# A graph kernel's second edge pass: which signal frees a ring row for the next gather

## The reference

```python
hh = (x @ W).reshape(n, H, D)                      # 8 heads of 32
s_src = jnp.einsum('nhd,hd->nh', hh, a_src)
s_dst = jnp.einsum('nhd,hd->nh', hh, a_dst)
scores = leaky_relu(s_src[src] + s_dst[dst], 0.2)
m = segment_max(scores, dst)
e = jnp.exp(scores - m[dst])
denom = segment_sum(e, dst)
msgs = hh[src] * (e / denom[dst])[:, :, None]
out = segment_sum(msgs, dst)
```

## Time and profile before

| what | value |
| --- | --- |
| median of 3 runs | 5405.28 us (5404.92 to 5430.75) |
| the profiled execution | 5400.45 us, its span 5398.4 us |
| this pass, first gather to last add | about 2797 to 4181 us of the span, 1384 us |
| busy share over the whole span | PE 73%, PEld 53%, DVE 57%, ACT 34%, POOL 46% |
| mean granted clock of TensorE | 0.844 of full speed |

### The profile page before, as it was taken

One profiled execution on the slowest core, in us unless ns is written; L12 is line 12 of the kernel. 1 busy time (PEld: TensorE's weight loads), 2 busy tenths in 40 slices (PEclk: granted clock), 3 DMA queues, 4 the chain that ended last, 5 costly groups with the idle time before them and its releaser, 6 DMA issues. The chain is left out here.

```text
span 5398.4 us, 69620 instructions
## 1 busy us (share of the span) xinstructions
PE 3959.7 (73%) x16281; PEld 2855.2 (53%) x16282; DVE 3059.0 (57%) x7623; ACT 1862.2 (34%) x5073; POOL 2462.0 (46%) x2442
## 2 busy tenths in 40 slices
PE   6867777777776659967854667666667338999999
PEld 4545555555554448856732444444444226777776
DVE  3278878778877766662063666666667773111111
ACT  1333433333333313211223444444444322333332
POOL 2256656556656450001166666666663422333332
PEclk8989988889989879987986776777777559999999
DMA  2555545455555332311173333333331451111111
GB/s 79 187 145 156 155 143 150 141 148 152 148 147 146 90 123 78 95 57 38 47 255 89 95 94 95 94 96 94 94 95 52 128 193 21 32 31 31 31 31 27
DMA packets 316127, 553.65 MB, mean 103 GB/s; under 512 B 63430, under 2 KB 213782, under 8 KB 315856
## 3 DMA queue, kind: packets, MB, share of 16 engines
q0 software_dynamic: 137120, 388.63, 26.5%
q1 hardware_dynamic: 178736, 161.98, 9.6%
HBM read 459.75 MB, written 90.62 MB: 102 GB/s over the span
## 5 line engine op out<-in xcount | busy, mean ns | idle before, releaser
L427 POOL DMA_INDIRECT attend_ring<-kv_rows,all_step_src x880 | 859.0, 976 | 630.0 <-PE attend_ps_agg L468 366.3
L942 POOL DMA_INDIRECT edge_ring<-head_rows,all_step_src x880 | 878.1, 998 | 455.6 <-issue 212.6
L978 PE MATMUL edge_ps_agg<-edge_msg,edge_sel 128*128 128x264 f32 x1760 | 727.3, 535 | 221.6 <-issue 65.4
L468 PE MATMUL attend_ps_agg<-attend_msg,attend_sel 128*128 128x264 f32 x1760 | 604.1, 445 | 188.1 <-DVE graph_qa L785 128.6
L978 PEld LDWEIGHTS edge_ps_agg<-edge_msg,edge_sel 128*128 128x128 f32 x1760 | 410.1, 259 | 373.6 <-issue 209.8
L2813 DVE TENSOR_TENSOR moe_gl<-moe_ps_h,moe_act 128x341 f32<-128x341 f32 x210 | 107.8, 514 | 776.8 <-PE moe_ps_h L2731 776.8
L452 PE MATMUL attend_ps_q<-graph_qa,attend_sel_t 128*128 x1760 | 525.8, 428 | 25.2 <-issue 25.2
L1283 DVE TENSOR_TENSOR graph_acc<-graph_acc,edge_ps_agg 128x264 f32 x880 | 369.6, 420 | 296.5 <-PE edge_ps_agg L978 195.4
L785 DVE SCALAR_TENSOR_TENSOR graph_qa<-graph_qa,all_step_same,attend_ps_agg 128x264 f32 x880 | 421.5, 479 | 176.0 <-remote 126.7
L468 PEld LDWEIGHTS attend_ps_agg<-attend_msg,attend_sel 128*128 128x128 f32 x1760 | 329.8, 209 | 352.5 <-issue 150.6
L2731 PE MATMUL moe_ps_h<-experts_w,moe_xt 128*128 x1680 | 501.8, 451 | 0.6 <-ACT moe_xt L2762 0.6
(11 more groups left out here) (424 smaller groups left out, 6470.4 us busy)
## 6 DMA issues: line engine op xcount, KB each, us to landing
attend_ring<-kv_rows,all_step_src POOLq DMA_INDIRECT x880
edge_ring<-head_rows,all_step_src POOLq DMA_INDIRECT x880
kv_rows<-qkv_kv SPq DMA_DIRECT2D x25, 512.0 KB, 2.9
experts_w<-in_w_t SPq DMA_DIRECT2D x16, 682.0 KB
attend_mask<-run_starts SPq DMA_DIRECT2D x440, 8.1 KB
edge_mask<-run_starts SPq DMA_DIRECT2D x440, 8.1 KB
head_rows<-hds_hh SPq DMA_DIRECT2D x25, 264.0 KB
qkv_x<-in_x SPq DMA_DIRECT2D x25, 256.0 KB, 3.2
```

The costliest lines, as they stand in the source:

```text
L427: nc.gpsimd.indirect_dma_start(ring[:, step % RING1, :], None, g.kv_rows, bass.IndirectOffsetOnAxis(g.step_src[:, step:step + 1], 0)).then ...
L468: nc.tensor.matmul(ps_agg[i % SUM_BANKS][:, 0:AGG], sel[:, q % 2, u % QU, :], msg[:, q % 2, u % QU, :], start=True, stop=True).then_inc(s_ ...
L942: nc.gpsimd.indirect_dma_start(ring[:, n % slots, u, :], None, g.head_rows, bass.IndirectOffsetOnAxis(g.step_src[:, step:step + 1], 0)).th ...
L978: nc.tensor.matmul(ps_agg[i % BANKS][:, 0:AGG], sel[:, q % 2, u % QU, :], msg[:, q % 2, u % QU, :], start=True, stop=True).then_inc(s_agg, 1)
```

## The change

In front of a gather whose row was used before, POOL waits for the count of messages of DVE instead of the count of sums of PE, with the same number, that of the step whose row it takes.

```diff
                 for u in range(CH):
                     step = n * CH + u
                     if n >= slots:
-                        pool.wait_ge(s_agg, step - slots * CH + 1)
+                        pool.wait_ge(s_msg, step - slots * CH + 1)
                     nc.gpsimd.indirect_dma_start(ring[:, n % slots, u, :], None, g.head_rows,
```

## The result

The changed kernel takes 5600.64 us, median of 4 runs (5578.69 to 5612.46), against 5410.62 for the kernel before (4 runs, 5404.92 to 5430.75): a ratio of 1.033, 95% interval 1.0307 to 1.0353. The profiled execution has 5578.69 us and a span of 5576.7. The forecast was 5405 us and no change.

What follows compares the result with a forecast made beforehand. The prediction took a ring of short hand-overs among PE, DVE and ACT, 23.9 us a turn, to bound the pass. Earlier gathers, the end and the new wait each counted 0, so 5405 us, range 5389 to 5421.

Steps and rivals of the forecast that it cites:

- rival 1: Each chunk from the fifth: stretched gathers make POOL the bound above a mean of 1.19 us; 5437 to 5595 us; 5%.
- one of 3: POOL's gathers: one hold of about 3 us in a chunk rather than two or three of about 1.3.
- the 3 us of the forecast: First reuse of a row: the gather starts at about 2900.6 in place of 2903.66, 3 us earlier.
- The lead of 24 us for the landings: Before L1183: the 464th gather is issued 24.1 us ahead; landing taken as 3.2 us, so earlier gathers gain 0.0 us.
- POOL's own pace of 20.8 us a turn: POOL's gathers: 16 of 1.000 us with 0.30 to the next take 20.8 of the turn's 23.9 us.
- The idle time of L942: POOL's gathers: about 418 us idle stays, released by DVE's L1271 in place of PE's L978.
- what the new wait costs: Pass: no one waits for the gathers behind the waiting one, DVE's messages don't slow; taken as 0, bound 16 us.
- a ring of hand-overs: Pass of the second graph: short hand-overs among PE, DVE and ACT set the turn of 23.9 us; none waits for POOL.
- the strange releasers: Waits before L1083 and L1203: rows name an early tensor and a DMA; prediction held that by code both wait for PE.
- Rivals 2 and 3: 2: a wait before L1203 hangs on gathers' landing, 5320 us, 2%; 3: message count held back, gathers unmoved, 5405 us, 4%.
- a shift in the hand-overs: Hand-overs of PE, DVE and ACT fall differently, without a nameable cause; remaining 2%, split between faster and slower.
- The range of 16 us on each side: DVE's messages and adds: 0.01 us either way for 16 of each in 51 turns, giving 5389 to 5421 us.

Runs made afterwards that it cites:

- b_plus4: Kernel before, but each gather waits for PE's sum of the step four later than its row's: 5040 us beside 5031, on the chip without late counts.
- a_mix4: Changed kernel, but the first gather of each four waits for PE's sum of its row, the others for the message: 5482 us beside 5481 before.
- a_no_gathers: Changed kernel without the 816 gathers behind the first 64: 5109 us beside 5455 for the kernel before.
- a_plain: Changed kernel, from the fifth chunk each gather is a plain load of 128 adjoining rows by POOL's queue: 5109 us beside 5481 before.
- a_sp: Changed kernel, from the fifth chunk SP's queue brings the same 128 adjoining rows by plain loads: 5117 us beside 5481 before.
- a_small: Changed kernel, from the fifth chunk each gather brings 66 numbers of a row in place of 264: 5628 us beside 5481 before.
- a_idx: Changed kernel, from the fifth chunk the gather's indices are 0 to 127 in order: 5608 us beside 5457 before.
- a_no_loads: Changed kernel with SP's loads of features, masks and flags for the first four chunks alone: 5606 us beside 5455 before.
- b_add: Kernel before, but the gather waits for DVE's add of its step instead of PE's sum: 5503 us beside 5455 before.
- a_pause8_more: Changed kernel with a pause of POOL (five small chained memsets) in front of every eighth gather: 5561 us beside 5407 before.
- b_plus8: Kernel before, but each gather waits for PE's sum eight steps later than its row's: 5040 us beside 5031, on the chip without late counts.

## Why the prediction was wrong

**The facts about POOL held.** The releaser is DVE; L942's mean is 976 ns, far from the 1.19 us of rival 1; nothing waits before L1183; a message still takes 410 ns as a mean; POOL's holds moved to DVE's messages, though 2.3 of them a turn of 3.3 us and not one of 3. The first reuse of a row follows the end of message 0 by 0.27 us (2906.03 to 2906.30), where it was 3.5 us, the 3 us of the forecast. The lead of 24 us for the landings was never used up. POOL's own pace of 20.8 us a turn is what b_plus4 runs at. The idle time of L942, forecast to stay, rose by 192 us since the turn grew. One reading was wrong and cost nothing: the message at 3502.32 does not lie between two gathers, as the next one starts at 3502.52, inside it. Over the whole pass before, the 770 messages that meet a gather and the 110 that don't both take 410 ns.

**The step that failed is the one on what the new wait costs**, and before it the reading of what bounds the kernel. It took the waits of ACT and DVE for PE as a ring of hand-overs of PE's work, and looked for harm only in what waits for a gather's landing or meets it at DVE's port. So the term for the new wait stood at 0, with 16 us for DVE's durations; it measured 177.0 us in the pass. It priced every count of PE as sent when PE had finished. In the trace of before one could have seen that they were not. L1083 waits 208.0 us and L1203 85.1 for counts of PE; the prediction put the strange releasers aside and never set such a start beside the end of PE's instruction. That one comparison (3503.56 to 3507.26) shows 3.7 us, where the first gather that waited for PE followed its sum by under 0.5 us. Where DVE waited for a late count, the count was 2.3 us late on average in the kernel before and 6.3 in the changed one. The wait that the change takes away was not needed for the data alone. It tied the gathers to the arrival of PE's counts (a_mix4 brings the time back with a quarter of the ties), and nothing in the prediction gave a price to a tie of that kind.

**The rivals.** Rival 1's time at its far end, 5595 us, is near what was measured, by chance: its mechanism, longer gathers, did not happen. Rivals 2 and 3 did not either. No gather of the changed kernel takes over 1.32 us. The 2% left for a shift in the hand-overs "without a cause that I can name" was where the outcome lay. The range of 16 us on each side came from DVE's durations alone and had no term for PE's counts; the miss is 196 us on the median.

**What is shown and what isn't.** Shown: counts of PE are raised late, by up to 8.8 us in the turn shown, and the idle time behind them has grown with the turn (timeline and raises); they come late because of POOL's indirect DMAs (a_no_gathers, a_plain, a_sp) and not of their bytes, their rows or SP's loads (a_small, a_idx, a_no_loads); a tie to PE in one gather of four was enough to return to the time of the kernel before, in one run (a_mix4). Argued only: that the tie works by stopping POOL just when a count is late. For it stand the 1.2 us between POOL's stop and the counts, and b_add between the two kernels; against its simple form stands a_pause8_more, where evenly placed stops do little. Open: what in the indirect DMA does it, whether PE's count or the last write of its sum is what is held up (PE's ends are modelled), and why one chip was free of it. No version that was run on a chip with late counts is faster than the kernel before; b_plus4 and b_plus8 were not run on one.

## What to carry to other kernels

Before a wait is taken from the engine that issues indirect DMAs, compare for a few hand-overs the end of the producer with the start of the consumer: where the gap is microseconds with the consumer idle, the signal is late, and a wait that looks needless may be what limits it. Here such a wait in front of one gather in four was worth as much as one in front of each. And run both versions on more than one chip, since the late counts that such a wait helps against may be absent on one.

## What the runs showed of the hardware that was not expected

- Where DVE stood idle before an add, it started 0.34 us (median) and at most 1.5 us after the modelled end of PE's sum without gathers, and up to 10.5 us after it in the changed kernel; in the turn shown two engines that wait for the same count go on within 0.11 us of each other.
- An indirect DMA of 128 rows keeps POOL for 946 to 960 ns as a median and 967 to 1008 as a mean, a plain one of the same bytes for 538.
- The granted clock of TensorE in the pass is 0.69 of full speed as a mean in the changed kernel, 0.73 to 0.74 in the one before and 0.90 in a_plain from 3000 to 3400 us; PE is busy 61, 68 and 73% of the time there, and a pass of its sums takes 544, 535 and 452 ns. Part of what the late counts cost may thus be paid in clock.
- One chip ran the kernel before in 5031 us, others in 5405 to 5481; on it, in each of four kernels, one add for which DVE stood idle started over 1 us after PE's end.
